# Banded attention on one core: projection chunks in three runs for each pair of heads, weight transposes of two heads side by side

## The reference

```python
qkv = x @ w_qkv                      # 256 -> 3 * 16 heads * 64
q = l2norm(q) * q_scale; k = l2norm(k) * k_scale
bq = rotary(q in windows * 8); bk, bv = look_around(k), look_around(v)
sim = einsum('bwid,bwjd->bwij', bq, bk)          # 128 x 384 for each window and head
sim = where(window_mask, NEG, sim)
out = einsum('bwij,bwjd->bwid', softmax(sim), bv)
x = layernorm(x + out @ w_out)
```

## Time and profile before

| | us |
|---|---|
| median of 3 runs | 3224.38 (3223.12 to 3226.81) |
| the profiled execution | 3225.97 |
| its span, first to last instruction | 3224.1 |
| PE busy | 3016.3 (94%) |
| DVE busy | 2384.7 (74%) |
| ACT busy | 2164.9 (67%) |
| POOL busy | 1649.6 (51%) |

### The profile page before, as it was taken

How to read it: one execution, slowest core, us unless ns; L and a number is a source line. 1 busy time by engine, 2 the same in 40 slices (tenths; PEclk the granted TensorE clock), 3 DMA queues, 4 the chain that set the end, 5 groups by cost and what they waited for, 6 DMA issues and landing times. The chain is left out here.

```text
span 3224.1 us, 70305 instructions
## 1 busy us (share of the span) xinstructions
PE 3016.3 (94%) x21167; PEld 2498.1 (77%) x21167; DVE 2384.7 (74%) x6865; ACT 2164.9 (67%) x5664; POOL 1649.6 (51%) x2222
## 2 busy tenths in 40 slices
PE   5999999999999999999999997799999999999986
PEld 4888788778778778778778785577888888888875
DVE  5877877877867867867867875687777777777764
ACT  4766666755755755756756764577788888778774
POOL 3655545645644644645645654344555554555455
PEclk9999999999999999999999999799999999999998
DMA  2000000000000000000000001200000000000000
GB/s 80 8 15 18 12 15 15 16 15 15 15 15 15 15 16 15 15 16 15 15 16 8 15 21 40 66 14 7 14 14 14 21 21 14 14 14 14 8 14 20
DMA packets 50150, 58.70 MB, mean 18 GB/s; under 512 B 2848, under 2 KB 47920, under 8 KB 49472
## 3 DMA queue, kind: packets, MB, share of 16 engines
q1 hardware_dynamic: 47056, 51.78, 5.1%
q10 hardware_dynamic: 2672, 1.87, 0.2%
HBM read 36.86 MB, written 16.78 MB: 17 GB/s over the span
## 5 line engine op out<-in xcount | busy, mean ns | idle before, releaser
L577 POOL TENSOR_SCALAR a_ex<-a_ex,a_rc 128x384 f32<-128x384 f32 (+1 forms) x1024 | 531.2, 532 | 753.9 <-DVE a_rc L489 753.5
L386 ACT ACTIVATE a_ex<-a_sm,a_nm 128x384 f32<-128x384 f32 (+1 forms) x1024 | 572.4, 560 | 100.8 <-DVE a_nm L482 97.8
L482 DVE CUSTOM_DVE_ANT_0 a_sm<-sc,a_mask,a_rn 128x384 f32<-128x384 f32 (+1 forms) x1024 | 531.6, 544 | 46.4 <-PE sc L267 44.2
L392 ACT ACTIVATE a_pt<-tp 128x256 f32<-128x256 f32 (+1 forms) x512 | 219.8, 429 | 306.1 <-PE tp L278 306.1
L1525 POOL TENSOR_TENSOR b_alo<-b_ring,b_ahi 128x512 fp32r<-128x512 f32 x128 | 169.2, 1322 | 469.7 <-DVE b_ring L1390 403.2
L236 PE MATMUL pj<-a_whi,a_xhi 128*128 128x384 f32 x1024 | 397.7, 388 | 2.5 <-DVE a_rb L460 2.5
L561 POOL TENSOR_TENSOR a_qr<-a_ra,a_rb 128x256 f32<-128x256 f32 x512 | 367.0, 731 | 36.8 <-DVE a_rb L460 36.6
L267 PE MATMUL sc<-a_kT,a_qT 64*128 64x384 f32 (+1 forms) x2048 | 346.4, 457 | 2.4 <-DVE a_nm L482 1.0
L236 PE MATMUL pj<-a_whi,a_xlo 128*128 128x384 f32 x1024 | 346.7, 339 | 0.0
L236 PE MATMUL pj<-a_wlo,a_xhi 128*128 128x384 f32 x1024 | 345.6, 337 | 0.0
L288 PE MATMUL qk<-a_pt,a_v 128*64 128x128 f32 x5120 | 314.6, 278 | 32.2 <-issue 21.8
(11 more groups left out here) (202 smaller groups left out, 8033.9 us busy)
## 6 DMA issues: line engine op xcount, KB each, us to landing
a_xin<-x SPq DMA_DIRECT2D x16, 512.0 KB, 3.9
a_xres<-x SPq DMA_DIRECT2D x16, 512.0 KB, 3.9
y<-a_res SPq DMA_DIRECT2D x16, 512.0 KB, 3.1
b_y<-y SPq DMA_DIRECT2D x16, 512.0 KB, 3.8
out<-b_y SPq DMA_DIRECT2D x16, 512.0 KB, 2.9
a_xin<-wqkv SPq DMA_DIRECT2D x8, 256.0 KB, 2.8
a_pt<-wqkv SPq DMA_DIRECT2D x1, 1536.0 KB, 6.9
a_ot<-wqkv SPq DMA_DIRECT2D x1, 1536.0 KB, 10.6
```

Source lines behind the costliest of these rows:

```text
L386: e.activation(ex[h][w][:, 0:width], sm[h][w % 2][:, 0:width], ACT.Exp, bias=nm[:, w, h:h + 1], scale=-1.0, accum_out=rs[:, w, h:h + 1]).t ...
L392: e.activation(pt[0][w][:, 0:width], TP[:, 0:width], ACT.Copy).then_inc(g['pt_act'], 1)
L482: e.tensor_tensor_reduce(out=sm[h][w % 2][:, 0:width], in0=SC[w % 2][h][:, 0:width], in1=mem['mask'][:, off:off + width], scale=rn[:, par, ...
L577: e.tensor_scalar(row, row, 0.0, rc[:, w, h:h + 1], ALU.add, ALU.mult).then_inc(g['exn_pool'], 1)
```

## The change

In `pe_half` the chunks of the projections and the weight transposes change places. In half 0 all four chunks of tiles 0 and 1 stand behind the first window's tw0 and tw1 and ahead of the k transposes. In half 1 three chunks (tile 2 and the first of tile 3) stand behind the first window's tw0 and tw1, and the last chunk behind the next window's. Half 1 of p=6 keeps its order, only written in loops. No other engine's code changes.

```diff
+        follows = at.has_next()
         if u == 0:
             if at.has_pair(1):
                 pe_q_transpose(e, n, n + 1, (p + 1) % 2)
-            pe_transpose_weights(e, i, w, 0, at.has_next())
+            for h in range(2):
+                pe_transpose_weights(e, i, w, h, follows)
             if at.has_pair(2):
-                pe_project(e, seq, n + 2, pair, w, 0)
-                pe_project(e, seq, n + 2, pair, w, 1)
-            pe_transpose_weights(e, i, w, 1, at.has_next())
+                for t in range(2):
+                    for c in range(DC):
+                        pe_project(e, seq, n + 2, pair, t, c)
             if at.has_pair(1):
                 pe_k_transpose(e, n + 1, (p + 1) % 2)
-            pe_transpose_weights(e, i + 1, w + 1, 0, at.has_next())
-            pe_transpose_weights(e, i + 1, w + 1, 1, at.has_next())
+            for h in range(2):
+                pe_transpose_weights(e, i + 1, w + 1, h, follows)
...
-        else:
-            pe_transpose_weights(e, i, w, 0, at.has_next())
-            if at.has_pair(2):
-                pe_project(e, seq, n + 2, pair, w, 0)
-                pe_project(e, seq, n + 2, pair, w, 1)
-            pe_transpose_weights(e, i, w, 1, at.has_next())
+                for c in range(DC):
+                    pe_project(e, seq, n + 2, pair, 2, c)
+                pe_project(e, seq, n + 2, pair, 3, 0)
             if at.at(0, 1) and not at.first:
                 pe_out_project(e, at.b - 1, 1)
-            pe_transpose_weights(e, i + 1, w + 1, 0, at.has_next())
+            for h in range(2):
+                pe_transpose_weights(e, i + 1, w + 1, h, follows)
             if at.has_pair(2):
-                pe_project(e, seq, n + 2, pair, w + 1, 0)
-            pe_transpose_weights(e, i + 1, w + 1, 1, at.has_next())
-            if at.has_pair(2):
-                pe_project(e, seq, n + 2, pair, w + 1, 1)
+                pe_project(e, seq, n + 2, pair, 3, 1)
```

More of the change, by code:

```diff
@@ L327, in pe_half @@
             if at.has_pair(1):
                 pe_k_transpose(e, n + 1, (p + 1) % 2)
-            pe_transpose_weights(e, i + 1, w + 1, 0, at.has_next())
-            pe_transpose_weights(e, i + 1, w + 1, 1, at.has_next())
-            if at.has_pair(2):
-                pe_project(e, seq, n + 2, pair, w + 1, 0)
-                pe_project(e, seq, n + 2, pair, w + 1, 1)
-        elif at.at(6, 1):
-            pe_transpose_weights(e, i, w, 0, at.has_next())
-            pe_transpose_weights(e, i, w, 1, at.has_next())
-            pe_transpose_weights(e, i + 1, w + 1, 0, at.has_next())
-            if at.has_pair(2):
-                pe_project(e, seq, n + 2, pair, w, 0)
-                pe_project(e, seq, n + 2, pair, w, 1)
-            pe_transpose_weights(e, i + 1, w + 1, 1, at.has_next())
-            if at.has_pair(2):
-                pe_project(e, seq, n + 2, pair, w + 1, 0)
-                pe_project(e, seq, n + 2, pair, w + 1, 1)
-        else:
-            pe_transpose_weights(e, i, w, 0, at.has_next())
-            if at.has_pair(2):
-                pe_project(e, seq, n + 2, pair, w, 0)
-                pe_project(e, seq, n + 2, pair, w, 1)
-            pe_transpose_weights(e, i, w, 1, at.has_next())
@@ new lines, in pe_half @@
+            for h in range(2):
+                pe_transpose_weights(e, i + 1, w + 1, h, follows)
+        elif at.at(6, 1):
+            for h in range(2):
+                pe_transpose_weights(e, i, w, h, follows)
+            pe_transpose_weights(e, i + 1, w + 1, 0, follows)
+            if at.has_pair(2):
+                for c in range(DC):
+                    pe_project(e, seq, n + 2, pair, 2, c)
+            pe_transpose_weights(e, i + 1, w + 1, 1, follows)
+            if at.has_pair(2):
+                for c in range(DC):
+                    pe_project(e, seq, n + 2, pair, 3, c)
+        else:
+            for h in range(2):
+                pe_transpose_weights(e, i, w, h, follows)
+            if at.has_pair(2):
+                for c in range(DC):
+                    pe_project(e, seq, n + 2, pair, 2, c)
+                pe_project(e, seq, n + 2, pair, 3, 0)
```

## The result

The changed kernel takes 3363.84 us (median of 5 runs, 3361.38 to 3366.38) against 3226.81 before in the same series: a ratio of 1.0423, 95% interval 1.0409 to 1.0438. That is 137 us where 119 were forecast, slower as forecast and inside the range.

The account below looks back on a forecast made before the run. PE was taken to bound the kernel, 98% busy in the attention stage. Ordinary pairs 94, p=5 10, p=6 9 and p=0 6 us sum to 119 us, giving 3344 us (3.7% slower); range 3285 to 3380, 8 in 10.

Parts of the forecast that it names:

- The kernel is bound by PE: Attention stage: PE is busy 98% of a 100 us window, so whatever makes PE wait lengthens the kernel.
- Fewer runs: Projection matmuls on PE: two runs fewer in a pair save about 0.02 us, 2 us in all, costed at nothing.
- kT 0.61 late: Half 0: k transposes start 1.04 us later, ACT covers 0.43; kT's copy and the chain behind it come 0.61 us late.
- The stall of tw1 in half 1: Half 1: tw1 waits for the mask maximum until 7.21, a 1.19 us stall; 81 pairs at 1.16 us make 94 us.
- the first score matmul of u=1 waits for this copy: Start of half 1 (u=1): scores wait for ACT's kT copy and start at 4.41 against 4.25 us.
- 0.4, 0.67 and 0.6 were forecast: Added us per pair in p=0 (late evacuation), p=5 (partly covered stall) and p=6 (late kT): 6, 10 and 9 us.
- "No wait" for tw1 in half 0: Half 0: tw1 moves to 0.71, behind the first maximum's read end at 0.54; no wait, cover 0.1 to 0.2 us.
- DVE didn't catch up: Rival at half 1's tw1: hidden ACT or DVE slack lets it start at 6.60; some 50 us, 3274 us; 7%.
- The clock stayed at its 2.4 GHz level: Rival: PE's clock falls in half 1, 1.65 us more in 96 halves, 158 us, about 3500 us; 4%.

## Why the prediction was right, and by how much it was off

**The kernel is bound by PE, and PE waits longer.** Right: equal busy time over the whole, a share of 92% in place of 98% of the window. **Fewer runs are worth nothing.** The run of twelve matmuls took 2.19 us (1069.53 to 1071.72), forecast 2.17: joining won or lost nothing that the times can tell. (The sum on record, 3225.97 + 119 less 1.6, is 3343 and not 3344; nothing hangs on that.)

**kT 0.61 late, and all of ACT's and DVE's chain with it.** The times were right to 0.05 us (kT at 3.69, maximum at 7.19), the cause was told too narrowly. Two things that ACT waits for stand behind the four chunks, kT and tw0 of the next window. With kT back in its place tw0 still held the last exponential and only some 10 us came back; with both back 37 did.

**The stall of tw1 in half 1.** The start of tw1 was right (7.25, forecast 7.21), the stall was not: it was to be 1.19 us in one place. The trace shows it in two. The scores came 0.79 late, which was forecast as 0.16, and that left about 0.6 for tw1 (tw0 at 1074.99, three transposes at 0.109, tw1 at 1075.92). In ordinary pairs the sum is the same, since the maximum sets the end, so the error didn't show there (1.04 or 1.17 in p=2 and 1.20 in p=7, forecast 1.16). That is luck: the forecast had no term for the wait of the scores.

**The step that failed** is "the first score matmul of u=1 waits for this copy". It waits for three things, and the last is DVE's evacuation of the second window's tw1, since that lies in SC[0][0], where the first score tile goes. Before, two chunks between that tw1 and the scores covered it. In p=0, 5 and 6 other PE work stands ahead of tw1, so nothing behind swallows the late scores: these pairs pay 0.95, 0.78 and 0.77 where 0.4, 0.67 and 0.6 were forecast. That is 0.83 us too little in a sequence, 12 in 15. That 0.67 and 0.6 come so near is luck too: they were for the maximum and for kT, but with the maximum moved ahead on DVE p=5 and 6 still take what they take in the change, and with a chunk of cover for the scores they take 0.5 us less.

**The cover that was too thin.** "No wait" for tw1 in half 0 rested on 0.1 to 0.2 us. In p=1 DVE makes the norm's statistics ahead of that maximum, and there PE now waits:

```profile
983.21 0.20 PEld L278 LDWEIGHTS sc<-s_ident,a_ex 128*128 128x128 f32 x2 [1.30 <-DVE a_nm L480]
```

Before, the k transposes of p=1 waited less for the same DVE work: PE idles 0.57 us there before and 1.07 ahead of tw1 now. That is the 0.45 us of p=1. But the thin cover alone doesn't make it: with half 0 alone in the new order p=1 costs 0.80 us, no more than p=7 (0.81), and DVE begins that maximum 0.91 us after the q transposes, as before; with half 1 alone p=1 costs 1.04 where p=7 costs 0.57, and DVE begins it at 1.27, as in the change. So the new order of half 1 brings DVE 0.36 us later to that maximum, and p=1 pays for this in either order of half 0. Pairs 3 and 4 are 0.15 and 0.13 above the forecast; absolute maxima delay DVE there, but that these are the cause was tried only in the kernel before. Together 11 us in 15 sequences. Against that, pairs at the edge of the loop, where PE waits some 4 us for other things, pay less than 1.16 in six of the rounds, by about 0.8 each (means of 17.71 before and 18.05 after), 5 us; these pairs scatter from 17.24 to 18.96 within the trace of before, so this part is uncertain. With the 12 of the scores this makes the 18 that were missing.

**The rivals.** DVE didn't catch up: its hole ahead of the reciprocal, a wait for ACT, shrank from 0.68 to 0.29 us, but the chain behind it still began 0.6 us late. The clock stayed at its 2.4 GHz level: 1.00 over the window, and 1.00 in the stretches of transposes and waits alone, 1.99 us in half 0 (1071.72 to 1073.71) and 1.23 in half 1 (1074.99 to 1076.22). The Trainium skill (TensorE: Matmul & The Clock Gate, Part 4: PE-mode transpose) says that transposes don't count as a busy PE in the same way. No loss of clock shows for it in this trace.

## What to carry to other kernels

Where one engine is full and others release its buffers, as here, the order of its work is the cover of its waits. Before moving work, list for each instruction every semaphore that it waits for, and ask of each what stood between the producer and it; the one that I passed over (a bank shared by transposes and scores) cost no less than the one that I priced: 89 us with half 0 alone, where the scores wait, against 58 with half 1 alone, where tw1 waits for the maximum. A wait that is taken away at one place may be found again one step on, as in the kernel before with its maximum moved: what helped there was to move work out of the chain that the waits follow, to where its engine waits anyway (9 us).

## What the runs showed that was not expected

A late instruction has more than one way to hold the chain behind it: with kT back at its old time (3.05 us) the chain on ACT was held by the next transposes instead, and only 0.17 us of the 0.61 came back at the maximum (its read ended at 7.02; 7.19 in the change). And the side-by-side order costs PE no work of its own: with most of its waits covered, the kernel that keeps three of four chunks in one run and the transposes of two heads side by side is 27 us (0.8%) slower than before at the same busy time of PE (3011.6 us; 3016.3 before). That the waits that are left make these 27 us wasn't tried.
